# A gated cross-attention block: PSUM banks divided three to one, and middle batches written out

## What is computed

```python
x = x + tanh(g_xattn) * xattn(layernorm(x), ctx, ctx, mask, ...)   # 16 heads of 32, relative bias
x = x + tanh(g_ffn) * ffn(layernorm(x), ...)

def xattn(query, key, value, ...):
    Q = (query @ Wq + bq).reshape(Bsz, S, 16, 32)                  # K, V alike
    scores = einsum('bqhd,bkhd->bhqk', Q, K) / sqrt(32)
    scores = scores + rel_bias[:, clip(q - k, -63, 63) + 63]
    scores = where(key_padding_mask, -inf, scores)
    return einsum('bhqk,bkhd->bqhd', softmax(scores), V).reshape(Bsz, S, 512) @ Wo + bo

def ffn(x, ...):
    x = x + attention(rmsnorm(x, w_ln1), ...)    # causal, latent keys and values, rotary halves
    return x + moe(rmsnorm(x, w_ln2), ...)       # 8 experts of which 2 are taken, one shared
```

## Time and profile before

| | |
|---|---|
| runs | 2403.45 us median of 3 (2398.34 to 2407.27) |
| the profiled execution | 2406.51 us |
| its span, first to last instruction | 2404.7 us |
| mean granted TensorE clock | 0.955 |
| TensorE matmul busy | 2139.2 us, 89% |
| VectorE busy | 1507.1 us, 63% |
| GpSimd busy | 1365.8 us, 57% |
| ScalarE busy | 1175.7 us, 49% |
| first attention, maxima matmuls from | 75.2 to 862.2 us |

### The profile page before, as it was taken

One profiled execution on the slowest core, in us unless ns is written; L12 is line 12 of the kernel. 1 busy time (PEld: TensorE's weight loads), 2 busy tenths in 40 slices (PEclk: granted clock), 3 DMA queues, 4 the chain that ended last, 5 costly groups with the idle time before them and its releaser, 6 DMA issues. The chain is left out here.

```text
span 2404.7 us, 49921 instructions
## 1 busy us (share of the span) xinstructions
PE 2139.2 (89%) x12672; PEld 974.7 (41%) x12673; DVE 1507.1 (63%) x4218; ACT 1175.7 (49%) x2316; POOL 1365.8 (57%) x1452
## 2 busy tenths in 40 slices
PE   3899999999999963899999999999985797899997
PEld 1333333333333311344444444444432443455554
DVE  3788888887888843566566566565544678344443
ACT  3355555555555442355545455454544474455554
POOL 4267677677677670265655565565651565455554
PEclk7999999999999986899999999999997899899999
DMA  5413323232232203443534344352414566666665
GB/s 176 146 60 102 104 81 117 71 106 91 93 107 76 84 5 130 146 121 117 152 93 135 119 135 124 99 155 89 140 43 137 112 153 133 107 114 114 113 110 90
DMA packets 222936, 264.57 MB, mean 110 GB/s; under 512 B 39192, under 2 KB 165004, under 8 KB 222388
## 3 DMA queue, kind: packets, MB, share of 16 engines
q1 hardware_dynamic: 197612, 212.79, 29.1%
q0 software_dynamic: 22976, 48.38, 11.5%
q10 hardware_dynamic: 2072, 0.28, 0.1%
HBM read 162.12 MB, written 86.80 MB: 104 GB/s over the span
## 5 line engine op out<-in xcount | busy, mean ns | idle before, releaser
L497 ACT ACTIVATE a_pt<-a_bank 128x512 f32<-128x512 f32 x512 | 305.1, 597 | 371.0 <-DVE a_bank L604 359.4
L1384 DVE CUSTOM_DVE_ANT_0 b_bank<-b_bank,b_tri 128x256 f32<-128x256 f32 (+3 forms) x512 | 253.9, 498 | 312.0 <-PE b_bank L1521 307.8
L615 DVE CUSTOM_DVE_ANT_0 a_bank<-a_bank,a_strip 128x512 f32<-128x512 f32 x512 | 354.1, 692 | 6.9 <-PE a_bank L758 4.3
L1169 POOL TENSOR_TENSOR b_acc<-b_acc,b_pt 128x256 f32<-128x256 f32 (+2 forms) x384 | 272.0, 726 | 102.4 <-ACT b_pt L1258 84.3
L407 POOL TENSOR_TENSOR a_acc<-a_acc,a_pt 128x512 f32<-128x512 f32 x256 | 317.2, 1272 | 8.0 <-ACT a_pt L497 4.3
L604 DVE TENSOR_TENSOR a_bank<-a_bank,a_band 128x256 f32<-128x256 f32 (+1 forms) x512 | 206.8, 405 | 136.6 <-PE a_bank L745 135.3
L1258 ACT ACTIVATE b_pt<-b_bank 128x256 f32<-128x256 f32 (+2 forms) x384 | 144.0, 383 | 204.7 <-PE b_bank L1505 194.1
L745 PE MATMUL a_bank<-a_q_stack,a_k_stack 128*128 128x512 f16 x512 | 196.8, 386 | 16.2 <-ACT a_pt L497 12.0
L758 PE MATMUL a_bank<-a_k_stack,a_q_stack 97*128 97x512 f16 x512 | 196.0, 383 | 3.8 <-DVE a_low L615 3.7
L1851 POOL DMA_INDIRECT out_dram<-c_z,c_to_row x72 | 114.1, 1585 | 137.1 <-DMA out_dram<-c_z,c_to_row 102.3
L1503 PE MATMUL b_bank<-b_q_stack,b_k_stack 96*128 96x256 f16 (+3 forms) x512 | 155.8, 304 | 10.6 <-issue 5.4
(11 more groups left out here) (346 smaller groups left out, 5449.4 us busy)
## 6 DMA issues: line engine op xcount, KB each, us to landing
b_q_stack<-qk_rows SPq DMA_DIRECT2D x192, 128.0 KB, 2.7
a_q_stack<-qk_rows SPq DMA_DIRECT2D x96, 128.0 KB
a_k_stack<-qk_rows SPq DMA_DIRECT2D x96, 128.0 KB
b_k_stack<-qk_rows SPq DMA_DIRECT2D x96, 128.0 KB, 2.6
a_sums<-in_x SPq DMA_DIRECT2D x34, 256.0 KB, 3.4
qk_rows<-a_qk_hi SPq DMA_DIRECT2D x64, 128.0 KB, 1.7
qk_rows<-a_qk_lo SPq DMA_DIRECT2D x64, 128.0 KB, 1.8
out_dram<-a_sums SPq DMA_DIRECT2D x32, 256.0 KB, 2.0
```

The source lines that it names most:

```text
L497: nc.scalar.activation(pt[:, n % SLOTS, :], st_bank[n % 2][:], ACT.Exp).then_inc(exped, 1)
L615: nc.vector.tensor_tensor_reduce(out=max_bank[step % 2][:], in0=max_bank[step % 2][:], in1=strip[:, g * HG + hh, at:at + S], scale=-1.0, s ...
L1169: nc.gpsimd.tensor_tensor(sums_of, sums_of, probs(n), ALU.add).then_inc(pooled, 1)
L1384: nc.vector.tensor_tensor_reduce(out=max_bank[step % 2][:, 0:w], in0=max_bank[step % 2][:, 0:w], in1=tri[:, at:at + w], scale=-1.0, scalar ...
```

## The change

The maxima get one bank (`a_bank0`) and the scores three (`a_bank1` to `a_bank3`) in the cross attention; the waits go with them, to the reduction of the step before and to the exponential of unit n - 3. In both attentions the loop over the steady batches becomes a Python loop, so that all six stand in the program with constants. Line numbers behind the first `over` fall by one, behind the second by two.

```diff
-        max_bank, st_bank, out_bank, job_bank = bank[0:2], bank[2:4], bank[4], bank[5:8]
+        max_bank, st_bank, out_bank, job_bank = bank[0], bank[1:4], bank[4], bank[5:8]
...
-            with eng.Fori(0, ROUNDS // 2) as i:
-                for u in range(2):
-                    body("steady", i * 2 + (1 + u), (1 + u) % 2)
+            for b in range(1, B - 1):
+                body("steady", b, b % 2)
...
-                        nc.scalar.activation(pt[:, n % SLOTS, :], st_bank[n % 2][:], ACT.Exp).then_inc(exped, 1)
+                        nc.scalar.activation(pt[:, n % SLOTS, :], st_bank[(b * UNITS + n) % 3][:], ACT.Exp).then_inc(exped, 1)
...
-                        nc.vector.tensor_tensor_reduce(out=max_bank[step % 2][:], in0=max_bank[step % 2][:],
+                        nc.vector.tensor_tensor_reduce(out=max_bank[:], in0=max_bank[:],
...
-                        if kind != "zero" or n >= 2:
-                            pe.wait_ge(exped, b * UNITS + n - 1)
-                        mm(st_bank[n % 2][:], k_stack[:, h, j * P:(j + 1) * P], q_stack[:, h, :], start=True,
+                        if kind != "zero" or n >= 3:
+                            pe.wait_ge(exped, b * UNITS + n - 2)
+                        mm(st_bank[(b * UNITS + n) % 3][:], k_stack[:, h, j * P:(j + 1) * P], q_stack[:, h, :], start=True,
...
-                        if kind != "first" or step >= 3 * GS + 2:
-                            pe.wait_ge(lowered, b * UNITS + step + (GS - 1))
-                        mm(max_bank[step % 2][:], q_stack[0:MASK + 1, h, i * P:(i + 1) * P], k_stack[0:MASK + 1, h, :],
+                        if kind != "first" or step >= 3 * GS + 1:
+                            pe.wait_ge(lowered, b * UNITS + step + GS)
+                        mm(max_bank[:], q_stack[0:MASK + 1, h, i * P:(i + 1) * P], k_stack[0:MASK + 1, h, :],
```

More of the change, by code:

```diff
@@ L603, in body @@
                         dve.wait_ge(scored, b * UNITS + n + 1)
-                        nc.vector.tensor_tensor(st_bank[n % 2][:, c0:c1], st_bank[n % 2][:, c0:c1], band[:, h, at:at + c1 - c0],
+                        nc.vector.tensor_tensor(st_bank[(b * UNITS + n) % 3][:, c0:c1], st_bank[(b * UNITS + n) % 3][:, c0:c1], band[:, h, at:at + c1 - c0],
                                                 ALU.add).then_inc(biased, 1)
```

## The result

The changed kernel takes **2526.93 us** (median of 4 runs, 2523.83 to 2529.89), the kernel before 2401.28 us beside it (4 runs): a ratio of 1.0519 [1.05, 1.0538]. The profiled execution took 2529.89 us with a span of 2527.8 us, 123.1 us longer than the span before.

A forecast was written before the change was run, and what follows sets the result against it. TensorE was taken to set the time. Against the profiled 2406.5 us, -13.5 (written-out batches) - 2 (third score bank) + 96 (steady batches) + 33 (ends) gave 2520, or 2517 us for the median; range 2451 to 2574.

The forecast's parts named there:

- the ends: First, next and last batch of the first attention: single maxima bank adds +9, +13, +11, together +33 us.
- the gain of the written-out batches: Both attentions: straight-line code removes branch gaps (10.57 us) and the slow clock after the last (3 us), -13.5 us.
- the steady batches: Six batches of the first attention: single maxima bank costs 16 us each (range 8 to 23), 96 in all.
- The chain: First attention's maxima: matmul, reduction and next matmul no longer overlap with one bank, 1.34 us a step.
- The walk: 16 steps of a steady batch followed through earlier trace rows: 4.45 us lost, 17.8 a batch.
- absorbed waits on the low halves: Steady batches: TensorE's present waits on VectorE's low halves, 2.6 us a batch, are partly absorbed, leaving 16 us a batch.
- One sign: Steady batches: TensorE waits for the reduction at most maxima matmuls, 13 us or more a batch.
- The third score bank: First attention: score matmul may start after exponential n-3, not n-2; -2 us, between 0 and -8.
- Rival (4): Third score bank stays unused because TensorE stands at the maxima matmul; price 2 us, counted within the forecast, no separate chance.
- (1): First attention: the maxima chain is hidden and the kernel is faster, 2388 us; chance 0.03.
- (2): First attention: only the bare 0.25 us in two steps of a run shows, +32, 2435 us; chance 0.07.
- (3): First attention: new gaps let the granted clock fall, adding 60 us, 2575 and more; chance 0.04.

The follow-up runs named there:

- two and two: Kernel before with the middle batches of both attentions written out, two maxima and two score banks kept: 2396.83 us, ratio 0.9964.
- the halved reduction: Changed kernel with VectorE's reduction over 256 of the 512 columns of the maxima bank: 2432.63 us, ratio 1.0122.

## Why the prediction was right, and where it was off

**The sign and the size.** Predicted 2517 us (2451 to 2574), measured 2526.93. The sum was +113.5 us against the profiled execution; the span grew by 123.1. The terms missed both ways: the ends were 8 us too small and the gain of the written-out batches some 4 us too large, and the steady batches, 3.5 us too large, gave a part of that back.

**The chain.** 1.34 us a step was worked out from the earlier trace rows, and 1.33 and 1.35 are measured. The walk gave 4.45 us for 16 steps, measured 4.49. Of 16 us a batch 15.4 came (116.5 for 101.1 in the kernels that differ in this alone), 92 for six where 96 stood. That the other three stretches are like the walked one did not hold. From the first maxima matmul of a steady batch on, the four stretches of 16 steps take 29.4, 30.9, 28.2 and 28.0 us for 26.4, 27.5, 23.6 and 23.6 with two and two: 2.9, 3.4, 4.6 and 4.4 more. The walk fits the two shorter stretches. In the two longer ones, the likely reason is that TensorE's longer steps hid more than VectorE's extra pieces added. Four times the walk is 17.8, and the 1.8 taken off for absorbed waits on the low halves brought it near: of these the lists of waits show 1.0 (2.5 us a batch with two and two, 1.5 with the single bank). One sign did not come as it was written: 13 us or more a batch of waiting for the reduction. The list has 8.2, since it hides what the modelled ends cover.

**The ends.** Predicted +33 for the single bank, measured 41: the first and zeroth batch 25.1 (133.7 for 108.6; 22 against the 111.4 and 111.5 of two other kernels with written-out batches), the last 16.1 (234.0 for 217.9), against 22 and 11. Together with the steady batches the bank's price is 133 us where the prediction had 129. These sizes were by eye, and the last batch was the one most under. In the changed kernel itself the first two batches cost 4 us more still (137.7), at a clock of 0.66 in its first 35 us for 0.76.
What the ends left out is the clock. The kernel with one maxima and two score banks shows both levels in its first batch, with nothing but the bare chain between these matmuls:

```profile
85.74 0.39 PE L757 MATMUL a_bank<-a_k_stack,a_q_stack 97*128 97x512 f16 x1 [0.96 <-DVE a_low L614]
...
89.01 0.61 PE L757 MATMUL a_bank<-a_k_stack,a_q_stack 97*128 97x512 f16 x1 [0.96 <-DVE a_low L614]
90.58 0.61 PE L757 MATMUL a_bank<-a_k_stack,a_q_stack 97*128 97x512 f16 x1 [0.96 <-DVE a_low L614]
```

The one at 85.74 is 1.35 us behind the one ahead of it; at the lower level the matmul takes 0.61 us and the step 1.57. So the first batch of the changed kernel took 24.8 us for its 16 steps, where 21 were predicted and 12.0 measured before. The last batch is at a lower clock as well, to its last score matmul 0.83 with the single bank and two score banks and 0.93 with two and two:

```profile
907.70:1019.80 112.10, 89.72 (x381) 21.86 (x379) 69.00 (x182) 46.23 (x83) 69.78 (x57) 0.83 0.12 36
```

```profile
789.80:885.70 95.90, 77.63 (x381) 22.13 (x379) 65.79 (x184) 46.34 (x84) 71.68 (x60) 0.93 0.14 45
```

Over both ends the lower level held for about 38 us more with the single bank. An estimate from these windows: if TensorE set the pace all that time, 19 of the 41 us would be the clock's. That is an upper bound, and no run separates the two.

**The third score bank.** -2 was predicted, between 0 and -8. The steady batches show none, and the medians no difference. Rival (4) held: in the steady batches TensorE stands at the maxima matmul and starts a score matmul 0.9 us or more after exponential n - 2, so the third bank is never what it takes. In the two traces the last batch and tail differ by 3.9 us in its favour and the first two batches by 4.0 us against it, and both differences go with the clock (0.89 for 0.83 in the last batch, 0.85 for 0.92 from 75 to 200 us).

**The written-out batches.** This term was off most for its size, next to the last batch: -13.5 predicted, -7.1 measured by the medians and -8.7 by the ratio. In the traces the gaps and the clock behind them went, and a little more (the steady batches 606.6 us for 611.4, the second attention 772.7 for 783.8, together -15.9). Against that stand +1.4 us in the first two batches and +4.8 in the third part, which the prediction did not price ("a few us at most" was its bound for a longer program). And the 10.57 us of gaps are those of one execution, on the high side: in another they were 9.4, and the two batches with the branch cost 10.0, 7.6, 3.8 and 3.1 us in four executions with the same second loop. A term read from one execution's stalls needs the range of several.

**The rivals.** (1) and (2), a hidden or half hidden chain: refuted by the 116.4. With a chain of 1.08 us rival (2) would have been near right, as the halved reduction shows. (3), the clock: not in the steady batches, whose new gaps of up to 1.3 us leave it at 1.00, so its 60 us did not come. But it came at both ends of the first attention. From 75 to 200 us the lower clock held for 37.5 us (window: 0.85) for 3.4 before, first in the first batch, where only maxima matmuls and products run, then twice in the zeroth; in the last batch for 25 us for 17. The trace of before, with the clock at 1.00 from 112 to 122 us at 6.5 of 10 busy, was a poor guide for that place. What the lower clock cost of the 30.5 us was not taken apart beyond the steps above.
The Trainium skill (TensorE: Matmul & The Clock Gate, A second HAM failure mode: psum-queue depth-cycling) describes a kernel that goes through PSUM banks in turn and whose TensorE is idle so often between groups of matmuls that the clock swings between both levels. The trace agrees in the first two batches, where the lower level came three times between 79.8 and 151.5 us, and does not in the steady ones, at 1.00.

**The branches.** The earlier trace rows and the repeat of the same kernel show gaps of 1.6 to 3.8 us for a taken branch (the first branch of the second attention has two). The Trainium skill (Runtime: NRT & Kernel Launch, Instruction fetch mechanics) says that a taken branch out of the fetched pages has to fetch its target first. The pages of the profile fit: instruction packets on one of the queues, before and in the changed kernel:

```profile
q14 instruction: 172, 1.41, 0.2%
```

```profile
q14 instruction: 100, 0.81, 0.1%
```

With one loop of the two written out it is 136 packets, halfway. That loops fetch their bodies again in each turn fits the three counts, but no run tried it by itself.

## What to carry to other kernels

Before a double-buffered bank is given away, work out the closed chain through the one that is left (producer, consumer, release) and set it against the shortest step, not the average one: here 1.34 us against 1.09, in a batch whose steps are 1.58 on average, cost 15 us a batch, and it cost more wherever the consumer's queue held a long piece between two turns. Buy a third bank only where the list of waits shows one on the second; here it showed none in the steady batches. If the batches are to be written out, leave the banks at two and two: that version, 2396.83 us, beats both kernels, by 0.4% and about 5%.

## What the runs showed that was not expected

- A taken branch costs 1.6 to 3.8 us of gap for the same code, and less with other code around it: two batches of a looped second attention lost 4.2 and 5.8 us in one kernel, 1.6 and 1.5 in another. Where it was cheapest, the gap stood in the list as a wait for ScalarE.
- With maxima matmuls 1.34 us apart at first (1.5 over the batch) and little else on TensorE, its granted clock was 0.66 and 0.76 over the first 35 us; with the halved reduction, 1.15 apart over the batch, 0.85; with two banks, 0.75 apart, 0.95. The lower clock also lengthens the step itself, from 1.35 to 1.57 us. Gaps of the same length among more matmuls left it at 1.00 for 580 us.
- The third part takes about 4 us longer (1.1 to 6.4 between single executions) when attention code ahead of it is written out. This stays open.
